# Attention and mixture of experts on one core: normalising the values in place after partition-picking DMAs, with the gate's columns behind the value weights

## What is computed

```python
qkv = x @ w_qkv                                    # 16 heads of 16
scores = einsum('bqhd,bkhd->bhqk', q / 4, k)       # causal
attn = softmax(where(causal, scores, -1e10))
out = einsum('bhqk,bkhd->bqhd', attn, v).reshape(b, s, 256) @ w_out
x = layernorm(x + out)
logits = x @ gate                                  # 32 experts, the top 4 of each token
h = x @ gate_up_proj[e]; g, u = split(h)           # inner width 96
y = sum over the chosen e of weight_e * ((u * silu(g)) @ down_proj[e])
x = layernorm(x + y)
```

## Time and profile before

| what | us |
|---|---|
| median of 3 runs | 477.55 |
| lowest and highest run | 477.39, 483.26 |
| span of the profiled execution, first to last instruction | 420.8 |
| what lies around the span (median less span) | 56.75 |

### The profile page before, as it was taken

How to read it: one execution, slowest core, us unless ns; L and a number is a source line. 1 busy time by engine, 2 the same in 40 slices (tenths; PEclk the granted TensorE clock), 3 DMA queues, 4 the chain that set the end, 5 groups by cost and what they waited for, 6 DMA issues and landing times.

```text
span 420.8 us, 10405 instructions
## 1 busy us (share of the span) xinstructions
PE 377.7 (90%) x2894; PEld 223.1 (53%) x2894; DVE 287.1 (68%) x1009; ACT 242.4 (58%) x534; POOL 235.4 (56%) x374
## 2 busy tenths in 40 slices
PE   5979999999999999997989899988999999989780
PEld 2526554444565445653444466665676777665230
DVE  1157767887879789889799489763666666643562
ACT  2431566667555776556857447562666666556842
POOL 5422144444223888227872855777777766646762
PEclk9999999999999999999999999996999999999987
DMA  4858555646751282649547435636655554429693
GB/s 137 261 192 231 172 165 173 189 136 209 213 164 29 90 277 91 190 144 276 176 149 224 138 123 149 189 132 195 188 175 169 165 158 145 129 69 369 235 375 118
DMA packets 54071, 74.78 MB, mean 178 GB/s; under 512 B 9842, under 2 KB 45308, under 8 KB 52480
## 3 DMA queue, kind: packets, MB, share of 16 engines
q1 hardware_dynamic: 46832, 56.93, 45.7%
q0 software_dynamic: 6912, 16.93, 11.0%
q10 hardware_dynamic: 272, 0.26, 0.2%
HBM read 46.33 MB, written 29.66 MB: 181 GB/s over the span
## 4 chain that ended last, share of the span: by engine, by line
PE 64%; DVE 16%; issue 7%; DMA 6%; ACT 3%; SPq 1%; POOL 1%; ACTq 0%; DVEq 0%
PE PS L697 12%; PE PS L868 8%; PE PS L719 7%; PE PS L821 6%; PE PS L790 5%; PE PS L847 5%; PE PS L665 5%; PE PS L804 3%; DVE MX L1425 2%; PE PS L928 2%; PE PS L710 2%; PE PS L898 2%; DMA YL<-scratch_y 2%; DMA scratch_qk<-PA 1%; DMA scratch_y<-Y,XG 1%
## 5 line engine op out<-in xcount | busy, mean ns | idle before, releaser
L1139 ACT ACTIVATE PT<-PS 128x512 f32<-128x512 f32 x160 | 92.0, 596 | 41.7 <-PE PS L847 36.9
L1783 POOL DMA_INDIRECT scratch_y<-Y,XG x80 | 79.5, 994 | 35.6 <-issue 18.2
L1755 POOL TENSOR_SCALAR_AFFINE_SELECT PT<-PT 128x256 f32<-128x256 f32 (+1 forms) x140 | 50.1, 367 | 78.0 <-ACT PT L1139 76.3
L1774 POOL DMA_INDIRECT scratch_slots<-XP,RI x64 | 63.8, 997 | 35.1 <-DVE XP L1368 16.1
L821 PE MATMUL PS<-KS,QS 96*128 96x512 bf16 (+3 forms) x256 | 61.7, 302 | 10.9 <-DVE MX L1432 4.6
L697 PE MATMUL PS<-W,XGT 128*64 x320 | 61.8, 337 | 1.2 <-DVE WG L1289 0.7
L847 PE MATMUL PS<-QS,KS 98*128 98x512 bf16 (+3 forms) x256 | 60.9, 299 | 1.5 <-ACT PT L1139 1.5
L699 PE MATMUL PS<-WG,XGT 128*64 128x192 f32 x320 | 61.9, 338 | 0.0
L1353 DVE SCALAR_TENSOR_TENSOR HH<-PS,XG,SG 128x96 f32<-128x96 f32 x80 | 24.9, 316 | 35.7 <-ACT SG L1061 31.0
L697 PEld LDWEIGHTS PS<-W,XGT 128*64 128x64 f32 x320 | 41.2, 139 | 13.7 <-issue 9.0
L821 PEld LDWEIGHTS PS<-KS,QS 96*128 96x128 bf16 x256 | 21.4, 99 | 44.7 <-DVE MX L1432 16.7
(11 more groups left out here) (237 smaller groups left out, 718.3 us busy)
## 6 DMA issues: line engine op xcount, KB each, us to landing
XG<-scratch_slots SPq DMA_DIRECT2D x160, 65.0 KB
scratch_qk<-PA SPq DMA_DIRECT2D x14, 384.0 KB, 3.4
W<-in_gate_up_dram SPq DMA_DIRECT2D x16, 288.0 KB
KS<-scratch_qk SPq DMA_DIRECT2D x32, 128.0 KB, 3.5
YL<-scratch_y SPq DMA_DIRECT2D x8, 512.0 KB, 7.0
QS<-scratch_qk SPq DMA_DIRECT2D x8, 384.0 KB, 3.7
QS<-scratch_qk SPq DMA_DIRECT2D x24, 128.0 KB, 3.6
W<-in_down_dram SPq DMA_DIRECT2D x8, 288.0 KB
```

The costliest lines, as they stand in the source:

```text
L1139: e.activation(PT[:, p % NPT, n, :], PS[:, 2 + (rank[u] - 1) % 2, :], ACT.Exp).then_inc(st_exp, 1)
L1755: e.affine_select(out=d, in_=d, compare_op=ALU.is_ge, fill=0.0, base=0, pattern=[[0, 1 if n < 2 else 2], [1, 128]], channel_multiplier=-1) ...
L1774: e.indirect_dma_start(out=XS[:, :], out_offset=bass.IndirectOffsetOnAxis(ap=RI[:, b % 2, TOPK * q + n:TOPK * q + n + 1], axis=0), in_=XP[ ...
L1783: e.indirect_dma_start(out=YK[:, :], out_offset=bass.IndirectOffsetOnAxis(ap=XG[:, j % NXG, D + 1:D + 2].bitcast(I32), axis=0), in_=Y[:, j ...
```

## The change

The unit "norm" and PE's part of "att" go. V holds each head's 16 values and 16 ones alternately, so that RAW has the outputs on even and the sums on odd partitions. A new unit ("spread", g), one slot after the quad's last pv, issues two DMAs of 64 partitions x 512 float32 each: even partitions of RAW to half of `AT[:, c]`, odd ones to the same half of a new tile `SU[:, c]`. ("att", b, c), four slots after every second spread, is now a reciprocal of SU (128x512) and a product of AT and SU (128x512), both on DVE and both in place. proj begins two slots after it. SP issues the spreads, ACT the last one. "xg" goes as well: the gate's 32 columns stand behind the value weights, "v" is one tile of 128 tokens and 288 columns, four per sequence, and ACT copies each in two instructions. The constant `onef` is 128x32; ones of 128x128 for `CS` are taken from V[1]. One load less (GT).

```diff
@@ make_plan
-        elif u[0] == "norm" and u[2] % 2:
-            put(slot + 3, ("att", u[1], u[2] // 2))
+        elif u[0] == "spread" and u[1] % 2:
+            put(slot + 4, ("att", u[1] // 4, u[1] // 2 % 2))
         elif u[0] == "att" and u[2]:
-            put(slot + 3, ("proj", u[1], 0))
+            put(slot + 2, ("proj", u[1], 0))
...
-                put(slot + 3, ("norm", b, n))
+                put(slot + 1, ("spread", g))
@@ build
+        def spread(e, g):
+            b, c, r = g // 4, g // 2 % 2, g % 2
+            e.wait_ge(raw_out, g + 1)
+            if b:
+                e.wait_ge(*full(("proj", b - 1, 3)))
+            for tile, first in ((AT, 0), (SU, 1)):
+                e.dma_start(tile[64 * r:64 * r + 64, c, :], RAW[first:128:2, r, :]).then_inc(spread_in[r], 16)
@@ tensor
-            idle = {("norm", B - 1, 3): 3, ("att", B - 1, 1): 4, ("proj", B - 1, 0): 3, ("place", B - 1): 14}
+            idle = {("spread", QUADS - 1): 8, ("att", B - 1, 1): 8, ("proj", B - 1, 0): 3, ("place", B - 1): 14}
...
+                    b, q = a
+                    wait_misc(e, u)
...
+                        t = e.matmul(PS[:, k, 0:VG], XT[:, b % 2, c, 128 * q:128 * q + 128],
+                                     WQ[:, c, 2 * D:2 * D + VG], start=(c == 0), stop=(c == 1))
...
-                elif kind == "norm":
-                    g = 4 * a[0] + a[1]
-                    wait_misc(e, u)
-                    e.wait_ge(raw_out, g + 1)
-                    for q in range(4):
-                        t = e.transpose(PS[:, k, 128 * q:128 * q + 128], RAW[:, g % 2, 128 * q:128 * q + 128],
-                                        idf[:, :])
-                    t.then_inc(done, 1)
...
-                    for c in range(2):
-                        e.wait_ge(*free(("att", b, c)))
+                    e.wait_ge(att_out, 2 * b + 2)
@@ scalar
+                    e.activation(V[b % 2][:, q, :, 0:2 * HD:2],
+                                 PS[:, k, 0:D].rearrange("p (h d) -> p h d", d=HD), ACT.Copy)
+                    e.activation(XL[:, b, q, :], PS[:, k, D:VG], ACT.Copy).then_inc(done, 1)
...
                     if g >= 2:
-                        e.wait_ge(*full(("norm", (g - 2) // 4, (g - 2) % 4)))
+                        e.wait_ge(spread_in[r], 32 * (g // 2))
                     e.activation(RAW[:, r, :], PS[:, 4 + r, :], ACT.Copy).then_inc(raw_out, 1)
@@ vector
+                elif kind == "att":
+                    b, c = a
+                    for r in range(2):
+                        e.wait_ge(spread_in[r], 32 * rank[u])
+                    e.reciprocal(SU[:, c, :], SU[:, c, :]).then_inc(sum_recip, 1)
                     e.wait_ge(sum_recip, rank[u])
+                    e.tensor_tensor(AT[:, c, :], AT[:, c, :], SU[:, c, :], ALU.mult).then_inc(att_out, 1)
```

More of the change, by code:

```diff
@@ L60 @@
 READY = {name: n + 1 for n, name in enumerate(CONSTS)}
-MISC = ("qk", "v", "xg", "wot", "wog", "sendmax", "norm", "att", "proj", "place", "count", "ends",
+MISC = ("qk", "v", "wot", "wog", "sendmax", "proj", "place", "count", "ends",
         "ecount", "eends", "etable", "lcount", "lends", "ltable")
+VG = D + NE
 def make_plan():
@@ L127, in make_plan @@
                 plan += [(kind, 0, m) for kind in ("qk", "resid", "part", "qkout")]
-            plan += [("load", 0), ("v", 0, 0), ("v", 0, 1)]
+            plan += [("load", 0), *[("v", 0, q) for q in range(4)]]
             for m in (1, 3):
@@ L132, in make_plan @@
             first = 5 * max(8 * b - 12, 0)
-            for c in range(2 if b > 1 else 0):
-                put(VALUES_AT[b - 2] + 2 * c, ("v", b, c))
+            for q in range(4 if b > 1 else 0):
+                put(VALUES_AT[b - 2] + 2 * q, ("v", b, q))
             if b == 1:
@@ L143, in make_plan @@
                     put(4 * n + 3, u)
-                for n, u in enumerate((("v", 1, 0), ("xg", 0), ("v", 1, 1))):
-                    put(2 * n + 12, ("half",) + u)
-                    put(2 * n + 13, u)
+                for q in range(4):
+                    put(12 + q, ("v", 1, q))
             for n, m in enumerate((0, 2, 1, 3) if b > 1 else ()):
@@ L593, in _ @@
                                 dwn[lo:lo + n].rearrange("x p n -> p x n")).then_inc(w_in, 16)
+                elif kind == "spread" and a[0] < QUADS - 1:
+                    g, = a
+                    if g == 2:
+                        e.wait_ge(max_free, 5 * PAIRS // B)
+                    spread(e, g)
                 elif kind == "nmout":
@@ L794, in _ @@
                 elif what == "v":
-                    b, half = a
-                    if 0 in parts:
-                        wait_misc(e, whole)
+                    b, q = a
+                    wait_misc(e, u)
                     e.wait_ge(wv_in, 16)
@@ L1144, in _ @@
                     if g >= 2:
-                        e.wait_ge(*full(("norm", (g - 2) // 4, (g - 2) % 4)))
+                        e.wait_ge(spread_in[r], 32 * (g // 2))
                     e.activation(RAW[:, r, :], PS[:, 4 + r, :], ACT.Copy).then_inc(raw_out, 1)
-                elif kind == "att":
-                    b, c = a
-                    e.wait_ge(*full(u))
-                    if b:
-                        e.wait_ge(*full(("proj", b - 1, 3)))
-                    e.activation(AT[:, c, :], PS[:, k, :], ACT.Copy).then_inc(done, 1)
+                elif u == ("spread", QUADS - 1):
+                    spread(e, QUADS - 1)
                 elif kind == "dev":
@@ L1801, in _ @@
                                 ALU.add).then_inc(pool_rows, 1)
-_INS = ["x", "xt", "w_qk", "w_v", "w_out", "gate", "gate_up", "down"]
+_INS = ["x", "xt", "w_qk", "w_v", "w_out", "gate_up", "down"]
 def laid_out(x, w_qkv, w_out, gate, gate_up, down):
@@ L1812, in laid_out @@
     w_qk = by_head.transpose(2, 1, 0, 4, 3).reshape(4, 128, 2, 128)
-    w_v = w_qkv[:, 2 * D:3 * D].reshape(2, 128, D).transpose(1, 0, 2)
-    return [_np.ascontiguousarray(a) for a in (x, xt, w_qk, w_v, w_out, gate, gate_up, down)]
+    w_v = _np.concatenate([w_qkv[:, 2 * D:3 * D], gate], axis=1).reshape(2, 128, VG).transpose(1, 0, 2)
+    return [_np.ascontiguousarray(a) for a in (x, xt, w_qk, w_v, w_out, gate_up, down)]
 def kernel(**inputs):
```

96 lines of the change are left out of this document (23 added, 73 removed).

## The result

| kernel | median of runs, us | span of the profiled execution, us | last "max" product begins | first expert product begins |
|---|---|---|---|---|
| before | 478.7 (4 runs) | 484.0 | 216.8 | 268.0 |
| after | 521.37 (4 runs, 518.55 to 522.26) | 518.8 | 250.3 | 305.0 |

The account below looks back on a forecast made before the run. Attention was taken to alternate between stretches set by PE and by DVE, PE at most two max units ahead. Terms -12.1 + 18.6 + 5 + 3.0 = +14.5 us gave 492 us, range 472 to 504.

Parts of the forecast that it names:

- The gate behind the values: PE in attention: gate products go (6.94 us), wider value products cost 1.7 us; net -5.2 us.
- The transposes: PE and DVE pieces of norm and att on the chain that ended last go: -6.8 us.
- rival D: Removed chain pieces had equal DVE work beside them, so half of the 12.1 us returns: +6, 498 us; chance 0.11.
- The reciprocal: DVE's reciprocal over 512 columns in att: 3.3 us, extrapolated from rows of 4 and 16 columns.
- The block of DVE: Att as one 4.1 us piece on DVE: four cost PE 2.6 us each, two their full length; +18.6 us.
- PE's clock: Granted clock read as full nearly throughout; no term for a fall behind new gaps in PE's work.
- The spreads' arrival: DVE waits for spreads queued on SP behind loads: 3 us at load 3, 2 for four others; +5 us.
- The tail: After the last quad's RAW, the last spread and 4.1 us of DVE delay proj(3,0): +3.0 us.
- A: Rival: a fast reciprocal of 0.69 us on DVE; -3.7 us, 473.9 us; chance 0.18.
- B: Rival: att's DVE block disappears in DVE's idle time, only the tail stays; -9.1 us, 468.5 us; chance 0.07.
- C: Rival: SP's queue makes all five odd spreads behind a load 3.5 us late, 17.5 us; 504.5 us; chance 0.12.
- The checks: Signs to look for, including PE's waits for maxima growing from 16.7 to some 35 us and gaps at each att.

Follow-up runs that it names:

- removals alone: Changed kernel with neither reciprocal nor product of att on DVE, proj waiting for the spreads' DMAs itself, att and proj later: 473.84 us, ratio 0.9873.
- blocks of one pass and covered gaps: Changed kernel with a one-pass product replacing the reciprocal, att and proj later, matmuls on constants in PE's gaps: 483.84 us, ratio 1.0115.
- fill taken out: Changed kernel with a one-pass product replacing the reciprocal, att and proj later, no matmuls in the gaps: 491.99 us, ratio 1.0171.
- att in its early place: Changed kernel with only the reciprocal replaced by a one-pass product, att and proj not moved: 500.94 us, ratio 1.0355.
- the filled run: Changed kernel with matmuls on constants in PE's gaps, 28 at the first and fourth att, 14 at the other four: 510.59 us, ratio 1.063.
- the second execution of before: The kernel before, unchanged, profiled again under the conditions of the timed runs: 483.65 us, ratio 0.999.

## Why the prediction was right or wrong

The runs give a ladder for the last max product: before 216.8; removals alone 210.7 (-6.1); with blocks of one pass and covered gaps 221.6 (+10.9); fill taken out 222.9 (+1.3); att in its early place 226.5 (+3.6); the reciprocal 250.3 (+23.8). The sum is +33.5. Steps of under 2 us in it are no more than the landmark's own scatter, and the step of 3.6 holds some 2 us of proj's work that changes sides. The step from 210.7 to 250.3, 39.6 us, can also be read by kinds: PE's gaps at the six att, 27.4 us, of which 7.0 are DVE's waits for spreads; PE's clock, 9.2 by the filled run; two proj products, about 2. That is 38.6. With the blocks at their whole length (24.6) in place of the gaps without the waits (20.4) it is 42.8. Both come near, so nothing large is missing, and the sum doesn't decide between the two.

*The gate behind the values, -5.2.* Right, as far as the landmark tells: -5.4 and -5.6 against the second execution of before, -3.3 and -3.5 against the first; the time is 1.0% shorter, some 5 us. The second copy of ACT cost nothing visible.

*The transposes, -6.8.* Failed. 3.0 us were there at 187 us, 0.5 at the last max product, so that of the -12.1 us of both removals -6.1 were left (-4.0 against the first execution of before). Adding pieces of PE on the chain that ended last took it for granted that PE keeps its pace without them. Part of it was taken back by a clock of 0.77 to 0.86 in the last stretch, which the forecast had at full; the rest was not there, and for that rival D's reason (equal work of DVE beside the pieces) is the natural reading, which no run tested by itself.

*The reciprocal, 3.3 us.* Right: 3.347 to 3.353, eight times. Two short rows with 4 and 16 columns carried a size 32 times larger:

```profile
L1417 DVE RECIPROCAL SU<-SU 128x512 f32<-128x512 f32 x8 | 26.8, 3351 | 25.6 <-DMA SU<-RAW 25.6
```

It comes to some 6.3 ns a column over the 147 ns that the forecast used as fixed cost, an estimate from this row. The Trainium skill's "VectorE: DVE Perf Modes", section "Walkthrough: the 8-slice pipeline in each mode", gives a repeat count of 8; read as eight cycles for each element that is an estimate of 4.3 us. The trace doesn't agree with that reading, nor with one result per cycle.

*The block of DVE, +18.6.* Undersized, though not by much. The rule was that PE's lead of two units pays for 1.5 us of a block wherever PE sets the pace. Without DVE's waits for DMAs, PE's gaps at the six att are 3.8, 3.2, 3.4, 3.3, 3.6 and 3.2 us, 20.4 in all. So four of them were larger than the 2.6 us of the rule and two smaller than the 4.1, and the stretches that were to be PE's and those that were to be DVE's don't differ. Three of the six stand at proj (L904), which waits for att itself. Whether a block costs its gap or its whole length (24.6 us in all) the runs leave open: added to the kernel before, 20.1 us of reciprocals cost 23.2 with the clock's fall, and where the gap was filled in time some 2.3 us each.

*PE's clock, not in the sum at all.* This is the step that failed by most. The earlier trace rows show the clock full, and the prediction kept it there while it opened gaps of 2.6 to 4.1 us in PE's work: it priced a gap by its length and put what comes behind it at nothing. In after the clock from 57 to 210 us is 0.91, and filling the gaps, which brought it to 0.99, gave back 9.2 us. What filling gives depends on the kernel: 9.2 us where the gaps are 3.4 to 7.2 us, 3.5 where they are 1.1 to 3.4 and one was missed, and 1.3 and 0.8, no more than scatter, where they are at most 4.3.

*The spreads' arrival, +5.* Nearly right in size: 7.0 us of waits before the last max product, 3.44 of them at load 3, where 3 was predicted from SP's queue, with load 3 in front exactly as read from the trace. The rest is a second late spread, 3.19 us, at the fourth att. What was wrong was the price: each wait prolongs the gap of PE, and the gap brings the clock down.

*The tail, +3.0.* From the last copy into RAW to proj(3,0) it is 289.6 to 298.50 us after and 258.3 to 263.54 before: 8.9 against 5.2, +3.7.

```profile
290.81 3.37 DMA SU<-RAW
...
294.28 3.36 DVE SU L1417
297.66 0.70 DVE AT L1419
298.50 4.19 PE PS L904 x8
```

The start came 4.3 us behind the landing, 4.1 predicted.

*The rivals.* A falls: with a fast reciprocal the kernel is still 3.6% slower. B falls: PE had its gap at each of the six att. C, 504.5, was nearest, but for a reason that was not so: two spreads were late, not five. D was right about the removal, in its size too (half of 12.1), and took the rest from the forecast's sum. None of them had the clock. The filled kernel, where most of the clock's fall is gone, is still 29 us slower than before (510.59 against 481.48), twice the forecast: the removals gave half and the gaps were larger, and some of the 29 us stays unexplained.

*The checks.* PE's waits for maxima were to grow from 16.7 to some 35: on PE's weight loads L1399, the L1432 of the earlier trace rows, went from 16.7 (15.3 in the second execution) to 24.6 and L1397, the L1430 of before, from 6.3 to 13.0, and the matmuls wait for the same two lines for another 13.0 + 8.7. The gap at each att was there, 7.23, 3.38, 3.39, 6.48, 3.61 and 3.35 us: 27.4 in all, where the sum had 23.6. The second, fourth and sixth are not in front of a max product, as predicted, but at proj.

## What to carry to other kernels

Don't count on the receiving engine's idle time for work that comes in one lump while the others run at most two units ahead of it: here DVE had 28 us of idle time, 20.1 us of reciprocals were added, and the last max product came 23.2 us later. A full granted clock in the profile of before is a resource that a new gap can spend: for each gap of PE that a change opens, ask what the matmuls behind it will cost at the lower level, and price it from rows. And of a change with two independent parts, measure each: here the small one, the gate's columns, gains 1.0% by itself and was hidden under the other. A filling of gaps has to be looked at in the trace before its result is read: in one run here a part of it came behind the gap and cost 4.47 us.

## What the runs showed of the hardware

A reciprocal of 128 x 512 float32 on DVE takes 3.35 us, a product by a constant of the same size in place 0.43 us, and a product of two such tiles 0.69 us. ACT's logarithm and exponential over the same tile take 0.63 us each, so the division by exp(-ln) costs 1.26 us and leaves DVE free; with att and proj later in the plan it brought the kernel from 1.084 to 1.011 of before.

Behind a gap of 7.23 us PE ran at its lower level (1.2 GHz) for 6.5 us; the fp32 products of L873 then took 1.51 us for sixteen instead of 0.86. Fourteen to 28 matmuls on constants in the gap kept the clock at 0.99. The lower level also came behind gaps of 1.81 us (0.61 us per matmul up to 192.8 us) and 3.72 us (0.39 us per matmul at 85.02, 0.61 at 86.77); behind one of 1.36 us in before it didn't, and once it came with no gap over 0.86 us in the 12 us ahead of it. What decides stays open.

Two profiled executions of the same kernel had spans of 420.8 and 484.0 us, 2.1 us apart at the last max product and far apart in the end of attention and the experts. Why is open as well.
